# Two gated layers of attention and feed-forward on one core: normalisations on ScalarE, held halves in DRAM, biases in the experts' products, new orders

## The reference, cut to what matters

```python
x = x + tanh(g_xattn[0]) * L0_xattn(_layernorm(x), ctx)   # 4 heads of 64: softmax(q k^T / 8) v, times Wo, plus bo
x = x + tanh(g_ffn[0])   * L0_ffn(_layernorm(x))          # x @ (W + up_aux @ lora_up @ lora_down @ down_aux)^T + b
x = x + tanh(g_xattn[1]) * L1_xattn(_layernorm(x), ctx, ctx)   # one head of 256, no scaling, biases bq bk bv
x = x + tanh(g_ffn[1])   * L1_ffn(_layernorm(x))
# L1_ffn: 16 heads of 16 of self-attention over the 112 rows, plus a mixture of experts:
gate = softmax(x @ W_gate + b_gate)                       # 8 experts
top_g, top_i = top_k(gate, 2)
combine = sum(one_hot(top_i, 8) * top_g[..., None])       # [rows, 8], two of them not zero
expert_out = einsum('bsd,edf->bsef', x, W_experts) + b_experts
moe_out = einsum('bsef,bse->bsf', expert_out, combine)    # all 8 experts are computed
```

## Time and profile before

| | |
|---|---|
| three runs | 920.3, 924.86, 925.35 us; median 924.86 |
| the profiled execution | 923.47 us, of it 921.5 span, from its first to its last instruction |
| TensorE's granted clock, mean | 0.977 |
| instructions | 34388 |
| PE, weight loads | 846.2 (92%), 666.0 (72%) |
| DVE, ACT, POOL | 785.2 (85%), 563.2 (61%), 392.7 (43%) |
| transfers | 61.82 MB, mean 67 GB/s |

### The profile page before, as it was taken

One profiled execution on the slowest core, in us unless ns is written; L12 is line 12 of the kernel. 1 busy time (PEld: TensorE's weight loads), 2 busy tenths in 40 slices (PEclk: granted clock), 3 DMA queues, 4 the chain that ended last, 5 costly groups with the idle time before them and its releaser, 6 DMA issues. The chain is left out here.

```text
span 921.5 us, 34388 instructions
## 1 busy us (share of the span) xinstructions
PE 846.2 (92%) x11764; PEld 666.0 (72%) x11764; DVE 785.2 (85%) x1910; ACT 563.2 (61%) x1230; POOL 392.7 (43%) x603
## 2 busy tenths in 40 slices
PE   4678999999999999999999999999999999999876
PEld 2467777778777777787777778777777787777654
DVE  3588989989998989899899998998999889888654
ACT  2444666666666666666666666666666666666443
POOL 3311545433455453344554433445544334454433
PEclk9789999999999999999999999999999999999987
DMA  7311222121112211212222122122221211111100
GB/s 257 114 61 57 66 79 66 59 73 61 58 61 75 75 62 62 68 57 63 64 75 74 52 73 63 53 70 66 75 70 54 75 60 56 61 59 56 39 6 6
DMA packets 41285, 61.82 MB, mean 67 GB/s; under 512 B 6158, under 2 KB 28036, under 8 KB 41128
## 3 DMA queue, kind: packets, MB, share of 16 engines
q1 hardware_dynamic: 41256, 61.43, 20.9%
HBM read 37.77 MB, written 3.67 MB: 45 GB/s over the span
## 5 line engine op out<-in xcount | busy, mean ns | idle before, releaser
L1317 POOL TENSOR_TENSOR acc<-part,acc 112x256 f32<-112x256 f32 x256 | 212.4, 830 | 298.9 <-DVE acc L1163 275.3
L820 ACT ACTIVATE part<-bankE,cgS 112x256 f32<-112x256 f32 x256 | 107.2, 473 | 3.0 <-PE bankE L329 2.3
L1266 POOL TENSOR_SCALAR ln_ve<-ln_mv 112x1 f32<-112x1 f32 x128 | 33.9, 265 | 174.5 <-DVE ln_mv L967 173.2
L329 PE MATMUL bankE<-wexs_hi,xT_hi 128*112 128x512 f16 x256 | 99.3, 388 | 3.4 <-ACT part L820 3.4
L1270 POOL TENSOR_TENSOR ln_rs<-ln_ve,cst 112x1 f32<-112x1 f32 x128 | 94.5, 738 | 10.7
L329 PE MATMUL bankE<-wexs_hi,xT_lo 128*112 128x512 f16 x256 | 97.7, 382 | 0.0
L329 PE MATMUL bankE<-wexs_lo,xT_hi 128*112 128x512 f16 x256 | 97.7, 382 | 0.0
L1067 DVE TENSOR_TENSOR p_lo<-p2T,p_hi 112x896 f16<-112x896 f32 x64 | 67.6, 1094 | 9.6 <-ACT p_hi L811 9.6
L1130 DVE TENSOR_REDUCE mx<-quad 112x8 f32<-112x896 f32 x64 | 69.6, 1088 | 1.0
L740 ACT ACTIVATE p0T<-quad 125x896 f32<-125x896 f32 x64 | 46.2, 722 | 38.6 <-PE quad L445 38.6
L973 DVE TENSOR_SCALAR xn<-x,ln_mv,ln_rs 112x256 f32<-112x256 f32 x96 | 54.9, 572 | 5.9 <-POOL ln_rs L1270 2.0
(11 more groups left out here) (239 smaller groups left out, 3275.5 us busy)
## 6 DMA issues: line engine op xcount, KB each, us to landing
ctf<-in_ctx_T SPq DMA_DIRECT2D x32, 375.0 KB, 3.1
ctn<-in_ctx_n SPq DMA_DIRECT2D x32, 375.0 KB
kvB<-kvA SPq DMA_DIRECT2D x32, 281.2 KB, 2.4
kc<-kvB SPq DMA_DIRECT2D x32, 187.5 KB
xin<-in_x SPq DMA_DIRECT2D x32, 112.0 KB, 2.0
x<-in_x SPq DMA_DIRECT2D x32, 112.0 KB, 2.1
out_x<-xout SPq DMA_DIRECT2D x32, 112.0 KB, 1.9
wex<-in_w_exp SPq DMA_DIRECT2D x1, 2048.0 KB, 9.9
```

The source lines that it names most:

```text
L329: last = mm(o, w, m, start=(n == 0), stop=(n == len(terms) - 1))
L820: act.activation(part[:, e, :], bankE[0:LQ, n * D:(n + 1) * D], ACT.Identity, scale=cgS[:, e:e + 1])\
L1317: pool.tensor_tensor(acc[:], part[:, 2 * j + n, :], acc[:], ALU.add).then_inc(moe_sum[j].sem, 1)
```

## The change

Stages go from five to six (F only finishes and stores). The parts:

- `normalise` moves to ACT, as one activation with scale rstd and bias -mean x rstd; POOL's `rstd` computes this shift with one more instruction.
- `kvB` is gone. SP writes `kvA` to a DRAM tensor `hold[b]` and reads kc0, kcA, kcB and kcm from it one stage later.
- The experts' biases become a seventh product in each pair's group. `combine_T`, `expert_bias`, `combine_copy`, `combine_lo` and `start_sum` are gone; POOL's sum begins with x3, each part taking up the sum of those before it.
- `gate_pick`, `gate_combine` and one scaling move from DVE to POOL, with tanh(g)/4096 made once at the start.
- Start: key and value weights come as two transfers, the key weights right behind the context; the low-rank product comes after the first projections, and its weights later.
- Every engine's order is new. PE's lap now begins at experts 3; taken as a ring, query_keys stands ahead of project_vg and scores1 ahead of project_qk, max1_T ahead of experts 0, scores1_T ahead of scores2, norm_T(0) ahead of experts 1, and norm_T(1) ahead of experts 2.

```diff
-            ts(xn[n][:], src[:], ln_mv[n][:, 0:1], ln_rs[n][:], ALU.subtract, ALU.mult).then_inc(ln[n].sem, 1)      (DVE)
+            act.activation(xn[n][:], src[:], ACT.Identity, bias=ln_sh[n][:], scale=ln_rs[n][:]).then_inc(ln[n].sem, 1)
...
             pool.tensor_tensor(ln_rs[n][:], ln_ve[n][:], minus_half, ALU.pow).then_inc(ln[n].sem, 1)
+            pool.wait_ge(ln[n].sem, ln[n].after("rstd", b))
+            pool.nop(nofuse=True)
+            pool.tensor_scalar(ln_sh[n][:], ln_mv[n][:, 0:1], ln_rs[n][:], -1.0, ALU.mult, ALU.mult).then_inc(ln[n].sem, 1)
...
-                if past(a - 1):
-                    sp.wait_ge(copyBC.sem, copyBC.after("m", a - 1))
-                sp.dma_start(kvB[:], kvA[:]).then_inc(copyAB.sem, DMA)
+                sp.dma_start(hold[a], kvA[:]).then_inc(held.sem, DMA)
...
-                sp.dma_start(kc0[:], kvB[:, 0:2, :]).then_inc(copyBC.sem, DMA)
+                sp.dma_start(kc0[:], hold[b, :, 0:2, :]).then_inc(fetched.sem, DMA)
...
                 group(bankE[0:LQ, 0:2 * D], [t for c in range(KD) for t in three(
                     h[:, c, :], l[:, c, :], wex_hi[:, c, cols].rearrange("p e n -> p (e n)"),
-                    wex_lo[:, c, cols].rearrange("p e n -> p (e n)"))]).then_inc(moe[j].sem, 1)
+                    wex_lo[:, c, cols].rearrange("p e n -> p (e n)"))]
+                    + [(ones16, bex[:, 2 * j * D:2 * (j + 1) * D])]).then_inc(moe[j].sem, 1)
...
-                    pool.tensor_tensor(acc[:], part[:, 2 * j + n, :], acc[:], ALU.add).then_inc(moe_sum[j].sem, 1)
+                    k = 2 * j + n
+                    pool.tensor_tensor(part[:, k, :], part[:, k, :], part[:, k - 1, :] if k else x3[:], ALU.add).then_inc(moe_sum[j].sem, 1)
```

More of the change, by code:

```diff
@@ L190, in flamingo_kernel @@
         vps = chain("vps", "ps hi lo")
-        ln = [chain(f"ln{n}", "stats mean_var var_eps rstd xn") for n in range(4)]
+        ln = [chain(f"ln{n}", "stats mean_var var_eps rstd shift xn") for n in range(4)]
         xTs = [chain(f"xT{n}s", "ps hi lo") for n in range(4)]
-        acc_s = chain("acc_s", "sum")
         qs = chain("qs", "ps hi lo")
@@ L381, in project_v @@
             def project_v(a):
+                if first(a):
+                    pe.wait_ge(wv_s.sem, wv_s.after("lo", 0))
                 if past(a - 1):
@@ L606, in values2, with body @@
                 last.then_inc(pv2.sem, 1)
[L608 to L641 removed]
+            def body(a, b, c, d, e, f):
+                A, B, C, DD, EE, FF = (v is not None for v in (a, b, c, d, e, f))
                 if EE: experts(3, e)
@@ L651, in body @@
                 if A: project_v(a)
+                if A: lora_1(a)
+                if C: query_keys(c)
                 if DD: project_vg(d)
-                if C: query_keys(c)
                 if B: values0(b)
+                if C: scores1(c)
                 if DD: project_qk(d)
-                if A: lora_3(a)
-                if C: scores1(c)
+                if C: max1_T(c)
+                if DD: experts(0, d)
+                if B: out0_T(b)
+                if C: scores1_T(c)
+                if A: lora_2(a)
+                if DD: scores2(d, a, b)
+                if B: project_o(b)
+                if A: lora_3(a)
+                if C: sums1(c)
+                if A: norm_T(0, a, bankB, wo_s, "x1", a - 1)
+                if DD: experts(1, d)
+                if DD: max2_T(d)
+                if A: layer1_A(a)
+                if C: out1(c)
+                if DD: scores2_T(d)
+                if A: project_q(a)
+                if B: norm_T(1, b, bankC, o1_s, "x3", b - 1)
+                if DD: experts(2, d)
+                if A: scores0(a)
             iterations(pe, body)
@@ new lines, in body @@
+                if EE: exp2(0, e)
+                if B: hi(qs, "ps", b, q_hi[:], cols(bankB, KD, LQ), 1 / SW, st0[1], "ps", b - 1)
+                if EE: exp2(1, e)
+                if C: xT_hi(1, c, bankC, f0_s, "ps")
+                if B: A_hi_copy(b)
+                if C: wex_hi_copy(3, c)
+                if EE: weigh_experts(2, e)
+                if C: bex_half(2, c)
+                if EE: probs2_hi(1, e)
+                if B: wf_hi(b)
+                if EE: probs2_hi(0, e)
+                if DD: normalise(3, x3, d)
```

512 lines of the change are left out of this document (243 added, 269 removed).

## The result

The changed kernel takes 910.42 us (median; 908.38 to 910.95), the kernel before 924.85: a ratio of 0.985 [0.982, 0.9879]. The forecast was 909 us and "faster". The total is right. Several of its terms are not (the price of the bias products, ScalarE's chain, the start), and the largest gain was credited to the wrong part of the change.

The account below looks back on a forecast made before the run. TensorE was taken to bound, with waits from VectorE's lateness. Per lap +0.63 - 1.20 + 0.25 = -0.32, times 31 is -10 us; with -4 at the start, 923.5 became 909.5, stated as 909; range 893 to 926.

Parts of the forecast that it names:

- TensorE bounds, and VectorE's lateness adds 1.2 to 1.6 us per lap: Steady lap of 26.44 us: TensorE limits, and nearly all its waits end on VectorE, said to be short of time.
- gain 0 on TensorE beyond what is counted: Halves held in DRAM instead of kvB: cost 0 and no separate gain for TensorE.
- VectorE's relief: VectorE loses four normalisations and eight more instructions, 4.5 us of about 24 per lap.
- Biases: +0.63: Four bias products add 0.86 us per lap on TensorE, combine_T and expert_bias going gives -0.23; nothing hides it.
- D: Rival: the bias products cost nothing because a wait was there anyway; lap 0.4 less, 895 us; chance 0.05.
- Waits: -1.20: TensorE's waits of 0.65, 0.15, 0.25, 0.07 and 0.08 per lap all go; bounds 0 to -1.29.
- All five: Waits before max0_T (0.65), ffn0 (0.15), norm_T2 (0.25), max2_T (0.07) and scores2 (0.08).
- The turnaround: +0.25, with 1.39 kept: Experts 2's last product to experts 3, sharing bankE, stays 1.39 us; a new 0.62 wait replaces 0.29 and about 0.08.
- Slack 0.2 to 0.3 us: ScalarE is ready to weigh experts 2 at 4.4 us after max2_T, TensorE ends them at 4.6; priced at nothing.
- The start: -4: project_k starts at about 8.6 us, 5.8 earlier, less some 2 us; bounds -6 and 0.
- Some 2 us come back: At the start, the low-rank chain between project_v and the first norm_T gives back about 2 us of the 5.8.
- rival B: GpSimd's shift late before rstd(1) delays ScalarE's queue and experts 3; lap 27.1, 940 us; chance 0.13.

Follow-up runs that it names:

- e9: The kernel before with only kvB replaced by a DRAM tensor that kc0, kcA, kcB and kcm are read from; 910.43 us in one run.
- e8: The kernel before with the old expert-bias path removed and a seventh product, of a zero tile, per pair of experts; 923.26 us in one run.
- e2: The changed kernel without the four bias products of the experts, biases left out of the result; 902.85 us in one run.
- e11: e1 with two unused 112x256 additions on GpSimd ahead of rstd(1); 928.42 us in one run.
- e10: e1 with TensorE's first product also waiting for the last of layer 1's weights; span 907.5 us, against 900.8 of e1.
- e1: The changed kernel with ctxT_hi moved ahead of max2_copy on ScalarE; 902.75 us, ratio 0.9757.
- e4: The changed kernel with the four normalisations back on VectorE, new orders kept; 915.62 us, ratio 0.9898.
- e7: e1 with 16 unread zero-tile products ahead of project_k and 8 behind the first batch's scores0; 902.21 us in one run.

## Why the prediction was right, and where it was not

**The total** came out 1.4 us from the forecast, with errors of opposite sign: laps 5 better than said, the end 1 better, the start 7 worse. That it came so close is luck. The waits that TensorE would lose were named in advance; what takes the largest of them away was not.

**What bounds the kernel.** "TensorE bounds, and VectorE's lateness adds 1.2 to 1.6 us per lap" was the reading of the earlier trace rows, and "Nearly all these waits end on VectorE, which is short of time, not idle" its reason. That the largest wait ends on VectorE is right, that it comes from a shortage of time is not. Of the 0.65 ahead of max0_T 0.49 was set by the chain copy out of kvB, copy into kvB, GpSimd's kvA, VectorE's kvA, max0 (e9). The row was there, in the earlier trace rows, and the text named it, and then priced the part at "gain 0 on TensorE beyond what is counted", while the gain was counted under VectorE's relief and the new orders. This is the step that failed in its attribution: 0.49 of the 1.20 belong to the part costed at nothing.

**Biases: +0.63.** The products run as forecast, 0.215 apart. Their price is not additive: in the kernel before 0.07 net was paid (e8), in the changed one their removal gives 0.24 of 0.86 (e2). What the forecast made a rival with a chance of 0.05 (D) is the case for two of the four in e8, and for 0.62 of the 0.86 in e2. The step that failed is "all on the bounding engine; nothing hides it": work added ahead of a wait and the same wait's removal were both counted in full, so the sum took +0.63 and -1.20 for what partly overlaps.

**Waits: -1.20.** All five are gone in the lap above, as said. The laps' error comes from no term alone: the sum said -0.32, the lap made -0.48.

**The turnaround: +0.25, with 1.39 kept.** Mis-sized: 1.58. The step that failed is ScalarE's chain, "Slack 0.2 to 0.3 us: priced at nothing, cover thin". From max2_T (409.16) it comes to the weighing of experts 2 after 4.8, not 4.4, and TensorE is done after 4.5, not 4.6. A normalisation there takes 0.60, not 0.45, which is 0.15 of this. The forecast took 0.42 from the row of `part`; that is half of a pair that overlaps (0.84). One instruction of `part` takes 0.47 in both kernels (median of 256: 474 ns). The 0.12 that remain go with its operands: `part` reads PSUM and has one pointer operand; the normalisation reads SBUF and has two. No run here parts the two. The Trainium skill, ScalarE: Activation LUTs, section "What ACT_TABLE_LOAD costs", gives 280 ns + 0.833 ns per column with a pointer bias, and 93 ns more for each further pointer operand. For 256 columns that is 0.59, an estimate by that page, and the trace agrees with 0.598.

**Halves in DRAM.** The page of the profile has the transfer land in 2.6 us (2.4 before), between the bounds of 2 and 5.

**GpSimd.** The shift is ready 0.3 before ScalarE wants it in the changed kernel (410.22 and 410.54; forecast 0.2), and what a delay costs is the forecast's chain in size (e11). Against that rival stood that no two-input subtraction of VectorE falls beside the additions; so it was in the steady lap. In the filling laps the rival did come true once, at 46.14 (see the start).

**The start: -4.** This is the term that failed: +3.1. project_k starts at 8.80 as forecast (8.6), 5.6 earlier than before, and by e10 a delay there counts in full. So some 8.7 us are lost between it and the first max1_T. "Some 2 us come back" was far too little. Rows of the start after:

```profile
15.02 0.59 PE L343 MATMUL bankE<-dax,ldT 100*4 100x256 f32 x2
...
17.34 1.31 PE L354 MATMUL bankD<-uaT,t 50*128 50x256 f32 x4 [0.47 <-ACT t L689]
19.28 0.61 PE L407 MATMUL bankB<-cst,xn 112*128 112x112 f32 x2 [0.63 <-ACT xn L843]
19.68 3.65 PE L334 MATMUL bankC<-l1k,l1q 128*128 128x256 f32 x8
...
26.26 0.53 PE L430 MATMUL quad<-k_hi,q_hi 64*112 64x375 f16 x4 [0.45 <-ACT q_hi L721]
```

The low-rank products, the first two of which ran ahead of project_k before, now stand in the path from 15.02 to 19.28. Layer 1's product takes 3.65 at the lower of the clock's levels (1.91 in e1, at the upper). Scores0 of batch 0 comes at 26.26, against 26.34 before: the lead is used up there. The 3.1 are lost after that, in three steps that the two traces show. Project_k of the second batch starts 0.6 later (33.78 and 33.19). In it and in project_v TensorE stays longer at the lower level, products of 256 columns still 0.21 apart where before they are 0.11. That is another 1.0 (a product of project_v stands at 38.36 and 36.81). The last 1.6 come between project_q and scores0 of the second batch. GpSimd, ScalarE and TensorE after, and TensorE before:

```profile
46.14 1.45 POOL L1256 TENSOR_TENSOR ln_rs<-ln_ve,cst 112x1 f32<-112x1 f32 x1
```

```profile
48.06 0.60 ACT L843 ACTIVATE xn<-x,ln_sh,ln_rs 112x256 f32<-112x256 f32 x1 [1.29 <-POOL ln_sh L1259]
```

```profile
48.80 0.60 PE L407 MATMUL bankC<-cst,xn 112*128 112x112 f32 x2 [1.41 <-ACT xn L843]
49.63 0.87 PE L430 MATMUL quad<-k_hi,q_hi 64*112 64x375 f16 x4 [0.22 <-ACT q_hi L721]
```

```profile
46.54 0.87 PE L423 MATMUL quad<-k_hi,q_hi 64*112 64x375 f16 x4 [0.66 <-ACT q_hi L711]
```

This is rival B's chain, in a filling lap. The power takes 1.45 beside VectorE's split of layer 1's weights (wqks_lo, 45.94 to 47.16, both inputs in SBUF), where the median is 0.57; the shift is late, ScalarE waits for it, norm_T(1) waits for ScalarE, and q_hi stands behind both the normalisation and ctxT_hi. No run changes this alone. With the normalisation on VectorE (e4) scores0 of the second batch starts at 47.08, but max0_T still waits for VectorE, and the first max1_T is only 0.6 earlier. That of e1 is 1.6 earlier, 0.7 of it there already at the first max0_T. How much of this is the order and how much the clock stays open: over the first 50 us and the next the granted clock was 0.86 and 0.94 before, 0.78 and 0.84 after, 0.84 and 0.86 in e1.

## What to carry to other kernels

A wait that ends on an engine need not be that engine's lack of time: follow it back through the instruction that waited ahead of it, here over two engines to a transfer whose own buffer was in use, and credit the gain to the part that takes this away. Product costs added and waits removed at the same place must not both be counted; walk the lap once with both. Half the length of a merged pair is less than one instruction alone: take the duration of a single one. An instruction whose inputs come early, standing in a chain without slack, is the cheapest thing to move (e1: one line, 8 us).

## What was not expected of the hardware

- ScalarE's activation of 112x256 takes 0.47 from PSUM with a pointer scale (two in a row 0.84), and 0.60 from SBUF with pointers for scale and bias; four of these per lap are 0.7 us more than half of the pair suggests.
- Moving 281.2 KB to DRAM lands in 2.6 us, from SBUF to SBUF in 2.4. In e9 the detour shows no cost, and it unties two buffers.
- Extra products at the start (e7) did not shorten the run: the mean granted clock was 0.969, in e1 0.972, and the 1.2 us won at the first max1_T were lost in the next lap.
- In the start TensorE issues the same products in the same order in the changed kernel and in e1, yet the first 26 us show a granted clock of 0.87 in one profiled execution and 1.00 in the other.
